# Non-local attention block: g through column tiles, and a new order of the half sums, the output projection and the peak of g

## The chip, the cores and the metric

One core of one Trainium2 chip. The metric is the time of one execution on the device in microseconds (us). The engines are TensorE (PE: matmuls; PEld: its weight loads), VectorE (DVE), ScalarE (ACT), GpSimd (POOL) and SyncE (SP), which here only issues DMAs. Each has its own queue and works it off in order; semaphores order them against each other.

## The reference

For each of 8 images x of shape 128 channels by 1024 positions:

```
g     = x^T w_g^T + b_g          (1024 x 64)
theta = x^T w_theta^T + b_theta  (1024 x 64)
phi   = w_phi x + b_phi          (64 x 1024)
att   = softmax(theta phi)       (1024 x 1024, over the last axis)
y     = att g                    (1024 x 64)
out   = x + batchnorm(w_out y + b_out)
```

## The kernel before, in words

An image has 8 tiles of 128 rows of att. The loop goes over tiles: step k issues work of several tiles at once, and every engine runs its own version of step k, written out by hand. j = k mod 8 is the *place* of a step in its image; the work of an image runs over into the next. Queues are in order, so the order of the lines of a step is the order of work. Of the 64 steps the first and last are written out singly, those between run in a loop of 16.

One tile t goes through: scores in place t-1 (TensorE, L721, four matmuls into one of two PSUM pairs of banks); row maximum (VectorE, L586, in the same place); exponential (ScalarE, L544, a place later), which frees the scores' banks for tile t+2; then turning (t+2). Tiles 0, 2, 3, 4 and 6 are turned on TensorE by eight transposes into the two banks of ps_flip (L786), read by ScalarE into an fp16 high part (pt_hi, L532) and by VectorE into a low part (pt_lo, L686); the next turned tile waits for the low part to free the bank. Tiles 1, 5 and 7 are split by GpSimd (L422, L426) and turned by DMA. VectorE corrects their row maxima by a small instruction (L591).

Four tiles are a *half*. y of a half is summed in one PSUM bank (ps_y): the *high-half matmuls* (sum_high, L733; 8 of 512 columns, 128 output rows) and two steps later the *low-half matmuls* (sum_low, L740; 8, each with 64 output rows, alternating between rows 0-63 and 64-127). The sums of the first half of an image stand in place 7 and, of the next image, 1; those of the second in 3 and 5 of the next image. VectorE then scales y (L603, places 2 and 6), TensorE projects it by w_out (convolve, L747, places 2 and 6, f32) into ps_misc, VectorE adds it to the residual (L596, places 3 and 7), SyncE stores it.

For the image after, three things are made in ps_misc too, one after the other: theta and phi (L811, places 0 and 1; ScalarE copies them out, L518), and g (project_g, L705, place 4: 8 f32 matmuls with 128 positions of x as weights and the 64 columns of w_g moving; ScalarE copies it to g_raw, L488). The largest absolute value of g sets its scale: VectorE reduces g along its rows (peak_of_g, L580, place 6), TensorE spreads the column of peaks over all partitions by a transpose (spread_peak, L727, place 7), VectorE reduces that (L655, place 0 of the next image) and derives factors (L658 to L664). GpSimd splits g into two fp16 parts (L430 to L439, place 3).

ps_misc has so many users that each waits for the last reader: the first projection of place 0 waits for the reduction of the spread peak (semaphore g_peak_read), g for the residual of place 3 (result_ready).

In a TensorE step the order before is: transposes of tile k-2; scores of tile k+1; theta and phi; output projection; g; high- or low-half matmuls; spread of the peak. On VectorE: reciprocals (places 0 and 4), scaled y, residual, peak, reduction of the spread peak, low part of tile k-2, row maximum of tile k+1.

Of the kernel before, what the change touches and what calls it, by code (L numbers as in the profile page):

```python
# [23 lines left out]
def build_nonlocal_attention(nc, x, w_tp_t, w_g_t, w_out_t, channel_vectors, out):  # L24
# [47 lines left out]
    with ExitStack() as ctx:  # L72
# [33 lines left out]
        g_raw = [sbuf(f"g_raw{i}", [P, MT, CI], F32) for i in range(2)]  # L106
# [59 lines left out]
        g_ready = sem("g_ready")  # L166
        g_out = sem("g_out")
# [96 lines left out]
        def _(sp):  # L264
# [68 lines left out]
            def image(it, k):  # L333
# [24 lines left out]
                turn_lo(MT * b + 1)  # L358
                inv_to_all(2 * b)
# [16 lines left out]
        def _(pool):  # L376
# [17 lines left out]
            def step(it, k):  # L394
# [33 lines left out]
                if j == 3 and exists(b, B) and not is_first(b):  # L428
                    hold(g_factor_ready, b + 1)
                    nc.gpsimd.tensor_scalar(out=g_parts[r][:, :, 0:CI], in0=g_raw[r][:, :, :],  # L430
                                            scalar1=g_factor[:, r:r + 1], scalar2=1.0,
                                            op0=ALU.mult, op1=ALU.mult).then_inc(g_hi_ready, 1)
                    nc.gpsimd.tensor_scalar(out=g_scaled[:, :, :], in0=g_raw[r][:, :, :],
                                            scalar1=g_factor[:, r:r + 1], scalar2=1.0,
                                            op0=ALU.mult, op1=ALU.mult).then_inc(g_scaled_ready, 1)
                if j == 3 and exists(b, B) and not is_first(b):
                    hold(g_hi_ready, b + 1)
                    hold(g_scaled_ready, b)
                    nc.gpsimd.tensor_tensor(g_parts[r][:, :, CI:2 * CI], g_scaled[:, :, :],  # L439
                                            g_parts[r][:, :, 0:CI], ALU.subtract).then_inc(g_split, 1)  # L440

                if j == 5 and exists(b + 2, B):
                    hold(g_ready, b + 2)
                    split_x(it * 16 + 16 * (k // STEPS + 2), r, 0)
                    split_x(b + 2, r, 1)
                if j == 7 and exists(b + 2, B):
                    split_x(b + 2, r, 2)

                if j == 1 and exists(b, B):
# [5 lines left out]
                    nc.gpsimd.tensor_scalar(out=resid[r][:, :], in0=x_in[r][:, :], scalar1=SHIFT, scalar2=1.0,  # L455
                                            op0=ALU.add, op1=ALU.mult).then_inc(resid_ready, 1)

# [27 lines left out]
        def _(act):  # L485
            def evacuate_g(b, source, target):
                wait(act, g_split, b - 1)
# [21 lines left out]
            evacuate_g(0, ps_flip[0][:, :], g_raw[0][:, :, :].rearrange("p t c -> p (t c)"))  # L509

            def step(it, k):
# [9 lines left out]
                if j == 5 and exists(image + 1, B):  # L521
                    act.wait_ge(g_ready, image + 2)
                    evacuate_g(image + 1, ps_misc[:, :], g_raw[(k // MT + 1) % 2][:, :, :].rearrange("p t c -> p (t c)"))
# [30 lines left out]
        def _(dve):  # L554
# [22 lines left out]
            def peak_of_g(b, r):  # L577
                dve.wait_ge(g_out, b + 1)
                wait(dve, g_peak_spread, b - 1)
                nc.vector.tensor_reduce(out=g_peak[:, r:r + 1], in_=g_raw[r][:, :, :], op=ALU.max, axis=AX.XY,  # L580
# [35 lines left out]
            def step(it, k):  # L616
# [24 lines left out]
                h = half_at(it, k - 11)  # L641
                if j % HALF_TILES == 3 and exists(h, HALVES - 2):
                    ring, part = (k - 11) // MT % 2, (k - 11) // HALF_TILES % PER_IMAGE
                    dve.wait_ge(resid_ready, image_at(it, k - 11) + 1)
                    add_residual(h, resid[ring][:, part * BANK:(part + 1) * BANK], ps_misc[:, :])
                if tile_is(it, k, 1):
                    peak_of_g(0, 0)
                if j == 6 and exists(image + 1, B):
                    peak_of_g(image + 1, (k // MT + 1) % 2)

                if j == (2 if is_first(image) else 0) and exists(image, B):
                    r = k // MT % 2
                    dve.wait_ge(g_peak_spread, image + 1)
                    spread = ps_y if is_first(image) else ps_misc
                    nc.vector.tensor_reduce(out=g_peak_all[:, r:r + 1], in_=spread[:, 0:P], op=ALU.max,  # L655
# [11 lines left out]

                if tile_is(it, k, 2):
                    dve.wait_ge(g_factor_ready, 1)
                    nc.vector.tensor_scalar(out=g_parts[0][:, :, 0:CI], in0=g_raw[r][:, :, :],  # L670
                                            scalar1=g_factor[:, 0:1], scalar2=None,
                                            op0=ALU.mult).then_inc(g_hi_ready, 1)
                if tile_is(it, k, 3):
                    dve.wait_ge(g_hi_ready, 1)
                    nc.vector.scalar_tensor_tensor(out=g_parts[0][:, :, CI:2 * CI], in0=g_raw[0][:, :, :],
# [18 lines left out]
            run_steps(dve, step)  # L694
# [6 lines left out]
        def _(pe):  # L701
# [68 lines left out]
            def step(it, k):  # L770
# [19 lines left out]

                t = tile_at(it, k + 1)
# [6 lines left out]
                if j in (0, 1) and more:  # L798
                    if j == 0:
# [4 lines left out]
                        if not is_first(image):  # L804
                            pe.wait_ge(g_peak_read, image + 1)
# [9 lines left out]
                if j % HALF_TILES == 2 and exists(h, HALVES - 2):  # L815
# [85 lines left out]
```

## Time and profile before

| | |
|---|---|
| median of 3 runs | 212.36 us (211.96 to 212.52) |
| the profiled execution | 212.18 us, of which the span is 210.4 us |
| granted clock of TensorE | 1.0 of full speed throughout |
| busy: PE / DVE / ACT / POOL | 198.5 / 178.4 / 136.8 / 152.4 us |
| DMA queue of SP | 35.01 MB, 81.2% of 16 engines |
| load of x, issue to landing | 3.3 us (median) |

The span runs from the first to the last instruction; some 1.8 us of the execution lie around it. Busy time is a sum over stages, and a busy PE counts the modelled tails of pipelined matmuls, so starts of instructions tell more than their lengths.

### The profile page before, as it was taken

The page shows a single profiled execution, that of the slowest core. Times are in us where ns is not written, and L with a number is a line of the kernel's source. Part 1 is how long each engine was busy: PE and PEld are TensorE (multiplying, and loading weights), DVE is VectorE, ACT ScalarE, POOL GpSimd, SP SyncE. Part 2 cuts the span into 40 slices and gives each one's busy share as a digit, 9 for nine tenths or more (in the row PEclk, how much of TensorE's full clock was granted, in tenths as well). Part 3 has the DMA queues.
Part 4 walks back from the last instruction along what each step waited for, and adds up shares of the span by engine and source line. Part 5 has one row for each costly group of instructions (what it writes and reads, how often), then busy time and mean ns, then how long its engine had stood idle before and what let it go on. Part 6 is the DMA issues. An engine that isn't in the chain of part 4 may idle for free.

```text
span 210.4 us, 3966 instructions
## 1 busy us (share of the span) xinstructions
PE 198.5 (94%) x1100; PEld 130.9 (62%) x1100; DVE 178.4 (85%) x291; ACT 136.8 (65%) x245; POOL 152.4 (72%) x127
## 2 busy tenths in 40 slices
PE   7996989999999998999999999999999998999993
PEld 6585856586565856577555955667565854566542
DVE  0789899978998799978999599978999699989871
ACT  2776866758575847767577666756578575658721
POOL 2448898699669998699778998699887964774400
PEclk9999999999999999999999999999999999999999
DMA  5215967999999998899959995899977997786111
GB/s 156 88 60 154 212 126 155 229 215 168 230 106 247 229 183 167 165 249 232 189 129 259 220 200 133 190 252 216 153 160 167 224 170 166 134 108 114 50 37 66
DMA packets 59500, 35.28 MB, mean 168 GB/s; under 512 B 50400, under 2 KB 50912, under 8 KB 59488
## 3 DMA queue, kind: packets, MB, share of 16 engines
q1 hardware_dynamic: 59200, 35.01, 81.2%
q10 hardware_dynamic: 288, 0.14, 0.2%
q14 instruction: 7, 0.06, 0.2%
q8 instruction: 5, 0.08, 0.2%
HBM read 8.36 MB, written 4.23 MB: 60 GB/s over the span
## 4 chain that ended last, share of the span: by engine, by line
PE 58%; DVE 15%; ACT 12%; issue 10%; DMA 2%; ACTq 1%; DVEq 0%
PE ps_scores L721 17%; PE ps_y L733 11%; PE ps_flip L786 9%; ACT probs L544 8%; PE ps_misc L705 6%; DVE neg_max L586 6%; DVE pt_lo L686 5%; PE ps_y L740 5%; ACT pt_hi L532 4%; PE ps_misc L747 3%; PE ps_misc L811 3%; DVE y_norm L603 2%; PE ps_scores L759 2%; DMA w_tp<-w_tp_t_dram 2%; PE ps_flip L705 1%
## 5 line engine op out<-in xcount | busy, mean ns | idle before, releaser
L544 ACT ACTIVATE probs<-ps_scores,neg_max 128x1024 f32<-128x1024 f32 x64 | 71.7, 1120 | 32.3 <-DVE neg_max L591 23.4
L586 DVE TENSOR_REDUCE neg_max<-ps_scores 128x1 f32<-128x1024 f32 x64 | 77.8, 1216 | 0.9 <-PE ps_scores L721 0.9
L686 DVE SCALAR_TENSOR_TENSOR pt_lo<-ps_flip,pt_hi 128x512 f16<-128x512 f32 x84 | 54.0, 685 | 15.8 <-ACT pt_hi L532 15.6
L532 ACT ACTIVATE pt_hi<-ps_flip 128x512 f16<-128x512 f32 x84 | 45.7, 596 | 20.4 <-PE ps_flip L786 20.1
L721 PE MATMUL ps_scores<-phi_hh,theta_hl 128*128 128x512 f32 x128 | 45.8, 439 | 5.2 <-ACT probs L544 4.8
L426 POOL TENSOR_TENSOR p_lo<-probs,p_hi 128x1024 f16<-128x1024 f32 x22 | 47.1, 2141 | 4.3 <-POOL p_hi L422 2.6
L786 PE MATMUL ps_flip<-ident,probs 128*128 128x128 f32 x336 | 45.0, 276 | 1.0 <-ACT probs L544 0.6
L786 PEld LDWEIGHTS ps_flip<-ident,probs 128*128 128x128 f32 x336 | 37.2, 142 | 11.6 <-issue 5.7
L721 PE MATMUL ps_scores<-phi_ll,theta_hl 128*128 128x512 f32 x128 | 40.1, 394 | 0.0
L422 POOL TENSOR_SCALAR p_hi<-probs 128x1024 f16<-128x1024 f32 x22 | 23.6, 1071 | 11.3 <-ACT probs L544 8.3
L721 PEld LDWEIGHTS ps_scores<-phi_hh,theta_hl 128*128 128x128 f32 x128 | 19.3, 190 | 18.9 <-ACT probs L544 17.5
L733 PE MATMUL ps_y<-pt_hi,g_parts 128*128 128x512 f16 (+1 forms) x128 | 30.0, 377 | 0.0
L721 PEld LDWEIGHTS ps_scores<-phi_ll,theta_hl 128*128 128x128 f32 x128 | 24.0, 188 | 5.6
L733 PEld LDWEIGHTS ps_y<-pt_hi,g_parts 128*128 128x128 f16 x128 | 11.4, 98 | 15.4 <-issue 4.2
L469 POOL TENSOR_TENSOR x_lo<-x_in,x_hi 128x512 fp32r<-128x512 f32 x14 | 17.8, 1276 | 0.8
L407 POOL TENSOR_TENSOR lo<-qk,hi 128x512 fp32r<-128x512 f32 x14 | 17.7, 1284 | 0.8
L603 DVE SCALAR_TENSOR_TENSOR y_norm<-ps_y,y_unit,inv_all 128x512 f32<-128x512 f32 x15 | 17.2, 1146 | 1.0 <-PE ps_y L740 0.9
L402 POOL TENSOR_SCALAR hi<-qk 128x1024 fp32r<-128x1024 f32 x7 | 7.4, 1051 | 13.8 <-ACT qk L518 13.8
L747 PE MATMUL ps_misc<-y_norm,wout 128*128 128x512 f32 x30 | 16.2, 620 | 0.7 <-DVE y_norm L603 0.7
L740 PE MATMUL ps_y<-pt_lo,g_parts 128*64 128x512 f16 (+1 forms) x128 | 16.7, 382 | 0.0
L705 PEld LDWEIGHTS ps_misc<-wg,x_in 128*128 128x128 f32 x112 | 13.6, 191 | 0.6
L705 PE MATMUL ps_misc<-wg,x_in 128*128 128x64 f32 x112 | 13.2, 271 | 0.0
(80 smaller groups left out, 176.8 us busy)
## 6 DMA issues: line engine op xcount, KB each, us to landing
x_in<-x_in_dram SPq DMA_DIRECT2D x16, 256.0 KB, 3.3
inv_all<-inv_row SPq DMA_DIRECT2D x15, 256.0 KB, 4.1
out_dram<-resid SPq DMA_DIRECT2D x15, 256.0 KB, 2.7
phi_hh<-hi SPq DMA_DIRECT2D x14, 256.0 KB, 5.2
phi_ll<-lo SPq DMA_DIRECT2D x14, 256.0 KB, 5.7
theta_hl<-hi SPq DMA_DIRECT2D x7, 256.0 KB, 4.3
theta_hl<-lo SPq DMA_DIRECT2D x7, 256.0 KB, 5.1
pt_hi<-p_hi SPq DMA_TRANSPOSE x22, 4.5
```

The lines of the kernel that those rows point to most:

```text
L422: nc.gpsimd.tensor_scalar(out=high[:, :], in0=p[:, :], scalar1=1.0, scalar2=0.0, op0=ALU.mult, op1=ALU.add).then_inc(p_hi_ready, 1)
L426: nc.gpsimd.tensor_tensor(low[:, :], p[:, :], high[:, :], ALU.subtract).then_inc(p_lo_ready, 1)
L532: nc.scalar.activation(pt_hi[ring][:, c * HALF_TILES:(c + 1) * HALF_TILES, slot * P:(slot + 1) * P], ps_flip[c][:, :].rearrange("p (a n) - ...
L544: nc.scalar.activation(probs[k % PROB_RING][:, :], ps_scores[k % 2][:, :], ACT.Exp, bias=neg_max[:, k % STEPS:k % STEPS + 1], accum_out=ro ...
L586: nc.vector.tensor_reduce(out=top, in_=ps_scores[k % 2][:, :], op=ALU.max, axis=AX.X, negate=True).then_inc(row_max_ready if by_dma(it, k) ...
L686: nc.vector.scalar_tensor_tensor(out=pt_lo[ring][where], in0=ps_flip[c][:, :].rearrange("p (a n) -> p a n", n=P), scalar=PROB_SCALE, in1=p ...
L705: last = nc.tensor.matmul(target[:, m * CI:(m + 1) * CI], x_in[r][:, m * P:(m + 1) * P], wg[:, :], start=True, stop=True)
L721: last = nc.tensor.matmul(ps_scores[k % 2][:, cc], theta_hl[r][:, cols], phi[:, cc], start=(n == 0), stop=(n == 1))
L733: nc.tensor.matmul(target[:, to], g_parts[r][:, m, :], pt_hi[ring][:, m, cols], start=(m == 0), stop=False, skip_group_check=True)
L740: last = nc.tensor.matmul(target[side * CI:(side + 1) * CI, to], g_parts[r][:, m, 0:CI], pt_lo[ring][:, m, cols], start=False, stop=(m >= ...
L747: nc.tensor.matmul(target, wout[:, 0:C], y_norm[:, cols], start=True, stop=True).then_inc(conv_ready, 1)
L786: last = nc.tensor.transpose(ps_flip[c][:, a * P:(a + 1) * P], probs[(k - 2) % PROB_RING][:, m * P:(m + 1) * P], ident[:, :])
```

## The change

- g is made with its channels on the partitions: two f32 matmuls with w_g as weights and 512 positions of x moving, the first into rows 0-63 of ps_misc, the second into rows 64-127 (two column tiles of the array), in place 5 behind the low-half matmuls. ScalarE copies this to g_channels, TensorE turns it back by four 128x128 transposes into ps_misc (place 6, behind the scores), ScalarE copies the result to g_raw (place 7). g_raw is one buffer instead of two, and the second copy waits for the split of the g before it.
- The high-half matmuls go ahead of the scores in their steps (places 3 and 7).
- The second output projection goes from place 6 to the end of place 7, its residual from place 7 to place 0, behind reciprocals and peak. The first projection of place 0 waits for this residual, no longer for the reduction of the spread peak.
- The peak of g goes from place 6 to place 0 of the next image, its spread to place 2 and into ps_y instead of ps_misc, the reduction to the head of place 3. The high-half matmuls of place 3, which write ps_y, wait for that reduction.
- GpSimd: input of the residual from place 1 to 3; split of g from 3 to 4; split of x from 5 to 6 (its last part stays in 7). SyncE: the store of the earlier image behind the turning DMA of a high part; the load of x behind the DMA of tile 1's low part. VectorE writes out 16 steps ahead of its loop instead of 8.

The core of the diff:

```
@@ SyncE, image(it, k)
-                store(it, k - 2 * MT + HALF_TILES)
                 inv_to_row(2 * b - 1)
                 turn_hi(MT * b - 1)
+                store(it, k - 2 * MT + HALF_TILES)
                 turn_lo(MT * b - 1)
-                if exists(b + 2, B):
-                    sp.wait_ge(g_ready, b + 1)
-                    sp.wait_ge(resid_ready, b + 1)
-                    load_x(b + 2, r)
...
                 turn_lo(MT * b + 1)
+                if exists(b + 2, B):
+                    sp.wait_ge(g_ready, b + 1)
+                    sp.wait_ge(resid_ready, b + 1)
+                    load_x(b + 2, r)
@@ ScalarE
-                wait(act, g_split, b - 1)
+                wait(act, g_split, b)
...
-                if j == 5 and exists(image + 1, B):
+                if j == 6 and exists(image + 1, B):
                     act.wait_ge(g_ready, image + 2)
-                    evacuate_g(image + 1, ps_misc[:, :], g_raw[(k // MT + 1) % 2]...)
+                    nc.scalar.activation(g_channels[:, :], ps_misc[:, :], ACT.Copy).then_inc(g_channels_out, 1)
+                if j == 7 and exists(image + 1, B):
+                    act.wait_ge(g_flipped, image + 1)
+                    evacuate_g(image + 1, ps_misc[:, :].rearrange("p (a c i) -> p a c i", c=PER_IMAGE, i=CI),
+                               g_raw[:, :, :].rearrange("p (c a) i -> p a c i", c=PER_IMAGE))
@@ VectorE, step
-                if j % HALF_TILES == 3 and exists(h, HALVES - 2):
...
-                if j == 6 and exists(image + 1, B):
-                    peak_of_g(image + 1, (k // MT + 1) % 2)
+                if j == 0 and exists(image, B) and not is_first(image):
+                    peak_of_g(image, k // MT % 2)
-                if j == (2 if is_first(image) else 0) and exists(image, B):
+                if j == (2 if is_first(image) else 3) and exists(image, B):
...
+                back = 11 if j == 3 else 12
+                h = half_at(it, k - back)
+                if j in (0, 3) and exists(h, HALVES - 2):
...
+                    add_residual(h, resid[ring][:, part * BANK:(part + 1) * BANK], ps_misc[:, :])
@@ TensorE, step, between the transposes of tile k-2 and the scores
+                h, quarter = half_at(it, k - 6), (k - 6) % HALF_TILES
+                if quarter == 1 and exists(h, HALVES - 2):
...
+                    if j == 3:
+                        pe.wait_ge(g_peak_read, image + 1)
+                    sum_high(ring, r, ps_y, slice(0, BANK), slice(0, BANK))
@@ TensorE, step, behind the scores
-                        if not is_first(image):
-                            pe.wait_ge(g_peak_read, image + 1)
+                        wait(pe, result_ready, 2 * image - 2)
...
+                if j == 2 and exists(image, B) and not is_first(image):
+                    pe.wait_ge(y_scaled, 2 * image - 1)
+                    spread_peak(image, k // MT % 2, ps_y[:, 0:P])
...
-                if j == 4 and more:
-                    pe.wait_ge(proj_out, 2 * image + 2)
-                    wait(pe, result_ready, 2 * image - 1)
-                    project_g(ps_misc, (k // MT + 1) % 2, range(MT)).then_inc(g_ready, 1)
+                if j == 6 and more:
+                    pe.wait_ge(g_channels_out, image + 1)
+                    for a in range(HALF_TILES):
+                        last = nc.tensor.transpose(ps_misc[:, a * P:(a + 1) * P],
+                                                   g_channels[:, a * P:(a + 1) * P], ident[:, :])
+                    last.then_inc(g_flipped, 1)
...
-                if j == 7 and more:
-                    wait(pe, result_ready, 2 * image)
-                    spread_peak(image + 1, (k // MT + 1) % 2, ps_misc[:, 0:P])
+                if j == 5 and more:
+                    pe.wait_ge(proj_out, 2 * image + 2)
+                    wait(pe, result_ready, 2 * image - 1)
+                    for c in range(PER_IMAGE):
+                        last = nc.tensor.matmul(ps_misc[c * CI:(c + 1) * CI, :], wg[:, :],
+                                                x_in[(k // MT + 1) % 2][:, c * BANK:(c + 1) * BANK],
+                                                start=True, stop=True, skip_group_check=True)
+                    last.then_inc(g_ready, 1)
+
+                h = half_at(it, k - 11)
+                if j == 7 and exists(h, HALVES - 2):
+                    if more:
+                        pe.wait_ge(g_out, image + 2)
...
+                    convolve(h, ps_misc[:, :], slice(0, BANK))
```

## Rows read from the trace of the kernel before

**Rows 1.** Chain of waits that ended last: shares of the span by engine.

```profile
PE 58%; DVE 15%; ACT 12%; issue 10%; DMA 2%; ACTq 1%; DVEq 0%
```

**Rows 2.** Timeline, TensorE: scores of tile 4 in images 0, 1, 7 (start, length, engine).

```profile
18.32 0.73 PE L721 MATMUL ps_scores<-phi_hh,theta_hl 128*128 128x512 f32 x2 [0.99 <-ACT probs L544]
...
40.62 0.73 PE L721 MATMUL ps_scores<-phi_hh,theta_hl 128*128 128x512 f32 x2
...
184.24 0.73 PE L721 MATMUL ps_scores<-phi_hh,theta_hl 128*128 128x512 f32 x2
```

**Rows 3.** Timeline, TensorE: a projection of image 1, places 4 to 4, images 3 and 4.

```profile
39.55 1.02 PE L747 MATMUL ps_misc<-y_norm,wout 128*128 128x512 f32 x2
39.98 0.59 PE L747 MATMUL ps_misc<-y_norm,wout 128*128 128x512 f32 x1
...
93.56 1.89 PE L705 MATMUL ps_misc<-wg,x_in 128*128 128x64 f32 x16
95.29 1.04 PE L786 MATMUL ps_flip<-ident,probs 128*128 128x128 f32 x8
...
97.19 1.05 PE L740 MATMUL ps_y<-pt_lo,g_parts 128*64 128x512 f16 x8
98.17 1.09 PE L786 MATMUL ps_flip<-ident,probs 128*128 128x128 f32 x8
99.02 0.71 PE L721 MATMUL ps_scores<-phi_hh,theta_hl 128*128 128x512 f32 x2
...
111.71 1.02 PE L747 MATMUL ps_misc<-y_norm,wout 128*128 128x512 f32 x2
113.01 0.73 PE L721 MATMUL ps_scores<-phi_hh,theta_hl 128*128 128x512 f32 x2 [0.28 <-ACT probs L544]
113.58 0.61 PE L721 MATMUL ps_scores<-phi_ll,theta_hl 128*128 128x512 f32 x2
114.04 1.90 PE L733 MATMUL ps_y<-pt_hi,g_parts 128*128 128x512 f16 x8
115.78 1.04 PE L786 MATMUL ps_flip<-ident,probs 128*128 128x128 f32 x8
```

**Rows 4.** Timeline, VectorE, the same stretch.

```profile
99.99 0.69 DVE L580 TENSOR_REDUCE g_peak<-g_raw 128x1 f32<-128x512 f32 x1
...
104.93 0.17 DVE L627 RECIPROCAL inv_sum<-row_sum 128x4 f32<-128x4 f32 x1
...
105.76 0.28 DVE L655 TENSOR_REDUCE g_peak_all<-ps_misc 128x1 f32<-128x128 f32 x1
...
107.59 1.21 DVE L586 TENSOR_REDUCE neg_max<-ps_scores 128x1 f32<-128x1024 f32 x1
...
108.94 1.22 DVE L586 TENSOR_REDUCE neg_max<-ps_scores 128x1 f32<-128x1024 f32 x1
110.08 1.13 DVE L603 SCALAR_TENSOR_TENSOR y_norm<-ps_y,y_unit,inv_all 128x512 f32<-128x512 f32 x1
111.41 1.29 DVE L686 SCALAR_TENSOR_TENSOR pt_lo<-ps_flip,pt_hi 128x512 f16<-128x512 f32 x2 [0.20 <-ACT pt_hi L532]
112.62 1.22 DVE L586 TENSOR_REDUCE neg_max<-ps_scores 128x1 f32<-128x1024 f32 x1
113.75 0.74 DVE L596 SCALAR_TENSOR_TENSOR resid<-ps_misc,bn,resid 128x512 f32<-128x512 f32 x1
114.41 1.22 DVE L586 TENSOR_REDUCE neg_max<-ps_scores 128x1 f32<-128x1024 f32 x1
115.54 0.17 DVE L627 RECIPROCAL inv_sum<-row_sum 128x4 f32<-128x4 f32 x1
```

**Rows 5.** Timeline, VectorE and TensorE, tiles 3 and 4 turned in image 0.

```profile
25.31 1.29 DVE L686 SCALAR_TENSOR_TENSOR pt_lo<-ps_flip,pt_hi 128x512 f16<-128x512 f32 x2 [0.79 <-ACT pt_hi L532]
...
26.14 1.16 PE L786 MATMUL ps_flip<-ident,probs 128*128 128x128 f32 x8 [0.18 <-DVE pt_lo L686]
...
27.06 0.71 PE L721 MATMUL ps_scores<-phi_hh,theta_hl 128*128 128x512 f32 x2
```

More of the change, by code:

```diff
@@ L105, in build_nonlocal_attention @@
         phi_ll = [sbuf(f"phi_ll{i}", [P, N], F32R) for i in range(2)]
-        g_raw = [sbuf(f"g_raw{i}", [P, MT, CI], F32) for i in range(2)]
+        g_channels = sbuf("g_channels", [P, BANK], F32)
+        g_raw = sbuf("g_raw", [P, MT, CI], F32)
         g_scaled = sbuf("g_scaled", [P, MT, CI], F32)
@@ L166, in build_nonlocal_attention @@
         g_ready = sem("g_ready")
+        g_channels_out = sem("g_channels_out")
+        g_flipped = sem("g_flipped")
         g_out = sem("g_out")
@@ L427, in step @@
                                             ALU.subtract).then_inc(p_lo_ready, 1)
[L428 to L449, printed above, removed]
+                if j == 3 and exists(b, B):
                     hold(shift_ready, 1)
@@ L456, in step @@
                                             op0=ALU.add, op1=ALU.mult).then_inc(resid_ready, 1)
+                if j == 4 and exists(b, B) and not is_first(b):
+                    hold(g_factor_ready, b + 1)
+                    nc.gpsimd.tensor_scalar(out=g_parts[r][:, :, 0:CI], in0=g_raw[:, :, :],
+                                            scalar1=g_factor[:, r:r + 1], scalar2=1.0,
+                                            op0=ALU.mult, op1=ALU.mult).then_inc(g_hi_ready, 1)
+                    nc.gpsimd.tensor_scalar(out=g_scaled[:, :, :], in0=g_raw[:, :, :],
+                                            scalar1=g_factor[:, r:r + 1], scalar2=1.0,
+                                            op0=ALU.mult, op1=ALU.mult).then_inc(g_scaled_ready, 1)
+                    hold(g_hi_ready, b + 1)
+                    hold(g_scaled_ready, b)
+                    nc.gpsimd.tensor_tensor(g_parts[r][:, :, CI:2 * CI], g_scaled[:, :, :],
+                                            g_parts[r][:, :, 0:CI], ALU.subtract).then_inc(g_split, 1)
+                if j == 6 and exists(b + 2, B):
+                    hold(proj_ready, 2 * b + 2)
+                    split_x(it * 16 + 16 * (k // STEPS + 2), r, 0)
+                    split_x(b + 2, r, 1)
+                if j == 7 and exists(b + 2, B):
+                    split_x(b + 2, r, 2)
             def split_x(count, r, part):
@@ L666, in step @@
                                             op0=ALU.mult).then_inc(y_unit_ready, 1)
+                back = 11 if j == 3 else 12
+                h = half_at(it, k - back)
+                if j in (0, 3) and exists(h, HALVES - 2):
+                    ring, part = (k - back) // MT % 2, (k - back) // HALF_TILES % PER_IMAGE
+                    dve.wait_ge(resid_ready, image_at(it, k - back) + 1)
+                    add_residual(h, resid[ring][:, part * BANK:(part + 1) * BANK], ps_misc[:, :])
                 if tile_is(it, k, 2):
                     dve.wait_ge(g_factor_ready, 1)
-                    nc.vector.tensor_scalar(out=g_parts[0][:, :, 0:CI], in0=g_raw[r][:, :, :],
+                    nc.vector.tensor_scalar(out=g_parts[0][:, :, 0:CI], in0=g_raw[:, :, :],
                                             scalar1=g_factor[:, 0:1], scalar2=None,
@@ L692, in step @@
                     row_maximum(it, k + 1)
-            run_steps(dve, step)
+            run_steps(dve, step, head=STEPS)
             dve.wait_ge(resid_ready, B)
@@ L814, in step @@
                 h = half_at(it, k - 10)
-                if j % HALF_TILES == 2 and exists(h, HALVES - 2):
+                if j == 2 and exists(image, B) and not is_first(image):
+                    pe.wait_ge(y_scaled, 2 * image - 1)
+                    spread_peak(image, k // MT % 2, ps_y[:, 0:P])
+                if j == 2 and exists(h, HALVES - 2):
                     if more:
-                        pe.wait_ge(*((proj_out, 2 * image + 2) if j == 2 else (g_out, image + 2)))
+                        pe.wait_ge(proj_out, 2 * image + 2)
                     else:
@@ L842, in step @@
                     spread_peak(0, 0, ps_y[:, 0:P])
-                if j == 7 and more:
-                    wait(pe, result_ready, 2 * image)
-                    spread_peak(image + 1, (k // MT + 1) % 2, ps_misc[:, 0:P])
+                if j == 5 and more:
+                    pe.wait_ge(proj_out, 2 * image + 2)
+                    wait(pe, result_ready, 2 * image - 1)
[8 more added lines that the diff above has]
+                        pe.wait_ge(g_out, image + 2)
+                    else:
+                        wait(pe, result_ready, h)
+                    convolve(h, ps_misc[:, :], slice(0, BANK))
                 if tile_is(it, k, TILES - 1):
```

25 lines of the change are left out of this document (9 added, 16 removed).

## The prediction

> **What bounds the kernel now.** I read the chain of waits first [rows 1]: TensorE holds 58% of the path that sets the end, VectorE 15%, ScalarE 12%. So TensorE is the first suspect, with the two others behind it in places. Next I asked whether the eight steps of an image repeat. The start of the scores of tile 4, in place 3 of the image, recurs at 40.62 us in image 1 and at 184.24 us in image 7, six images later: 143.62 us, or 23.94 us per image; from image 0 to image 1 it is 22.30 us [rows 2]. Then I read one such image on TensorE [rows 3] and on VectorE [rows 4] in order of time. TensorE issues almost without a gap: the largest in the rows is 0.28 us ahead of the scores of tile 4, where it waits for an exponential. VectorE is also nearly full between 104.93 and 115.54 us. The reader is to see that neither engine has much room: a change that makes each wait for the other once per image turns two nearly full engines, side by side, into two that run partly in turn. That is what I shall count.
>
> **Prices of what is moved** (start to start, so that pipelined tails are not counted twice). Scores of a tile 1.03 (113.01 to 114.04); high-half matmuls 1.74 (114.04 to 115.78); low-half matmuls 0.98 (97.19 to 98.17); eight transposes of a tile 0.85 (98.17 to 99.02); the old g projection 1.73 (93.56 to 95.29) [rows 3]. On VectorE: row maximum 1.13 (112.62 to 113.75), with its correction for a tile turned by DMA 1.35 (107.59 to 108.94), low part of a turned tile 1.21 (111.41 to 112.62), residual 0.66 (113.75 to 114.41), reciprocals in place 0 0.83 (104.93 to 105.76), peak of g some 0.6 (0.69 less the tail), reduction of the spread peak 0.28 [rows 4].
>
> **g itself.** It removes 1.73 us on TensorE and adds two f32 matmuls of 512 columns and four transposes. The nearest row for the matmul is the output projection: two instructions, the second starting 0.43 after the first [rows 3]. So there are four instructions of 0.43. If the two column tiles ran wholly side by side they would take 0.86, if not at all 1.72. That column tiles do overlap is in rows 3: eight low-half matmuls, alternating between the two column halves, take 0.98, where eight high-half ones of the same column count take 1.74. But here both instructions of one half are issued before both of the other, so only the middle two are neighbours on different halves; I take three times 0.43, 1.3. The transposes are half of a tile's eight, 0.43. Sum 1.73: nothing won, with ends at -0.44 and +0.42 per image.
>
> On the order of such instructions the Trainium skill has two rules: "TensorEngine Tiling (Array Packing)", Key Properties, lets different tiles run matmuls in parallel, which alone would give 0.86; "TensorE: Matmul & The Clock Gate", What overlaps and what doesn't, says that matmuls start and end strictly in program order, which gives the 1.3. No row here shows two pairs in this order, so both ends stay open; seven images of g make the difference 3 us.
>
> **One step later for g (place 4 to 5).** In place 4 g stood between the scores of tile 5 and the transposes of tile 3, and covered the time in which VectorE made the low part of tile 2, which the transposes wait for (same PSUM bank). Without the cover the wait is seen. In image 0 it once stands bare: the low part starts at 25.31, the transposes at 26.14, the next scores at 27.06 [rows 5], so the transposes can start 0.83 and the next scores 1.75 after it. Price below, in the sum.
>
> **High-half matmuls ahead of the scores (places 3 and 7).** No work is added, but the scores of tiles 4 and 0, and so their row maxima, come 1.74 later. Before, VectorE worked on those maxima while TensorE did the high half [rows 3, 4]; now it has to stand still.
>
> **The spread peak through the bank of y.** The transpose moves to place 2 and its reduction to the head of VectorE's place 3, and the high-half matmuls of place 3 (which clear that bank) get a wait for it. In the old image the output projection of place 2 starts at 111.71 and ends by 112.73; VectorE is through place 2 only at 113.75 [rows 3, 4]. Add 0.28 for the reduction and some 0.05 for the signal: TensorE would start the high half at about 114.1, 1.35 after it is free. Queued behind that wait are the scores of tile 4, and on them VectorE itself. This is the step on which the forecast rests.
>
> **Second output projection and residual (places 6 and 7 to 7 and 0).** Same work. The first projection of place 0 now waits for the residual, which on VectorE stands behind row maximum, reciprocals and peak: 1.13 + 0.83 + 0.6 + 0.66 = 3.2 after the maximum of tile 0 starts. TensorE gets there at 2.6 (from 1.18 before: scores 1.03, projection 0.86, transposes 0.85, scores 1.03), so it waits 0.6; but the maximum of tile 2, which needs the scores behind it, is not due on VectorE until 5.8, so this costs nothing on the path. Without that cover it would cost those 0.6.
>
> **ScalarE, GpSimd, SyncE.** A second copy of g, some 0.6 us like the first, lands in place 7, where ScalarE waits for VectorE; the first copy takes the place of the old one, behind g. The transposes of g wait for it, but turning tile 4 and the scores of tile 7 (0.85 + 1.03) cover it. On GpSimd residual input, g split and x split move later by one or two places, in the same order of dependence; on SyncE the load of x goes behind a turning DMA. I cost these at nothing either way. The split g is wanted by the high half of place 7, three places on. The load of x is issued at place 3 and its split stands in place 6, behind the parts of tile 5: three places of some 3 us (23.94 / 8) against a landing of 3.3 us (the profile's table). The unrolled VectorE steps cost nothing.
>
> **The sum, around the loop.** Start at the scores of tile 4. Row maximum can begin 1.18 later (113.01 to the end of the second row, 113.58 + 0.61 [rows 3]), takes 1.13, reciprocals 0.35 (0.17 in rows 4, and a scaling of like length): low part of tile 2 at 2.66. Scores of tile 6 at +1.75 [rows 5]: 4.41. Scores 1.03, low half 0.98, g 1.3, transposes of tile 4 0.85, scores 1.03, transposes of g 0.43, high half 1.74: scores of tile 0 at 11.77, its maximum at 12.95. From there VectorE is the path: 1.13 + 0.83 + 0.6 + 0.66 + 1.21 (low part, tile 6) + 1.35 + 1.14 (maxima 1 and 2) + 1.33 (scaled y with the wait behind it, 110.08 to 111.41) + 1.21 + 1.13 [rows 4] + 0.33 for the reduction and signal = 10.92. High half 1.74, and the scores of tile 4 are due again: 25.6 us, against 23.94. The stalls that this hides in TensorE are 0.8 at tile 3, 0.6 at place 0 and 1.1 at place 3; VectorE's are about 1.3 ahead of maximum 0 and 1.9 ahead of maximum 4.
>
> Five such images give 5 x 25.6 = 128.0. The last of the six has no projections and so none of the wait behind the scaled y: 25.3. Together 153.3 against 143.6: +9.7. Image 0 has no low half and no residual yet: 25.6 - 0.98 - 0.66 = 24.0 against 22.3: +1.7. Behind tile 4 of the last image 1.74 less is queued, as the high half is already done; VectorE holds the low part of tile 2 back until 2.66, so I estimate 1.4 back. Sum +10.0. The profiled execution took 212.18 (the median of the runs shown is 212.36): 222.2, and with the 0.2 between them 222.4. I round down to 222, as the wait behind y may shrink when VectorE is later.
>
> **Rivals.**
> 1. *g's column tiles don't overlap as counted.* Wholly beside each other: 0.44 less per image, 3 us, 219. Not at all (the change doesn't do what it says): +0.42, 225. For the first speaks the low half's 0.98, for the second that both instructions of one half stand together.
> 2. *Only the wait of place 3 is paid.* If the late maxima of tiles 4 and 0 find other slack, what is left per image is the bare 1.1 less the 0.28 that the scores of tile 4 no longer wait: +0.8, seven times, less 1.4 at the end, +4.4, 216.5. Against it: VectorE's rows show no such slack [rows 4].
> 3. *Faster.* TensorE stays the bound and the freed time is kept. Place: place 3, at the new wait. If VectorE reaches place 3 before TensorE ends the output projection, no stall arises, the high half fills the 0.28 that was idle, and with g at 0.86 each image costs 0.72 less: seven times, -5, 207. It decides when VectorE is 1.35 us earlier against TensorE than in the old image; for it speaks that peak and residual leave places 6 and 7, against it that they are put into place 0, ahead of place 3, on the same engine.
> 4. *No change.* Waits paid only where TensorE waited before; nothing in the rows favours it.
>
> **How the numbers follow.** Forecast with the rivals of g near it (218.5 to 225) 0.62; rival 2 and other partial cover (214 to 218.5) 0.16; above 225 0.08; within 0.3% (0.6 us, about what a measurement of this kernel tells from no change) 0.04; faster 0.10. The range from 215.5 to 226 takes in the forecast's own 218.5 to 225 (0.62), most of rival 2 (0.12) and most of what lies above (0.05). Slower by over 0.3%: 0.86.
>
> **What would show it.** A wait of the high-half matmuls in place 3 for the reduction of the spread peak, 1 us or more in each of seven images; VectorE idle ahead of the row maxima of tiles 4 and 0; transposes of tile 3 waiting for the low part of tile 2; an image of 25 to 26 us. g from its first matmul to the next transposes tells its overlap: 0.9, 1.3 or 1.7. I am wrong if VectorE reaches the reduction before TensorE asks for it.

## The result: 5.6% slower, and the profile after

The changed kernel takes 223.85 us (223.04 to 225.51, 4 runs) against 212.44 (211.96 to 212.77) for the one before on the same chip: ratio 1.056, 95% interval 1.052 to 1.059. 222.0 was forecast, with 215.5 to 226. The profiled execution took 224.01, 11.83 more than the profiled one of before. Where a kernel below had one run over 1.5% above its fastest (e4, e5, e12), its median holds that run and its ratio leaves it out.

Shares of the chain that ended last, and the busy row, after:

```profile
PE 195.6 (88%) x1044; PEld 126.0 (57%) x1044; DVE 179.2 (81%) x291; ACT 142.7 (64%) x252; POOL 152.3 (69%) x127
...
PE 53%; DVE 23%; issue 9%; SPq 4%; DMA 3%; POOL 3%; ACT 2%; DVEq 1%; POOLq 0%
```

VectorE has nearly the same work as before (179.2 us against 178.4), but its share of the path rises from 15% [rows 1] to 23%. The reader is to see that no engine got slower; engines wait for each other. The waits after (who waited for whom: us in total, times, longest us):

```profile
DVE neg_max L592 <- PE ps_scores L728: 24.6, 16, 1.9
...
POOL x_hi L466 <- DMA x_in<-x_in_dram: 11.4, 7, 3.5
...
PE ps_y L740 <- DVE g_peak_all L655: 8.0, 7, 1.4
...
PE ps_misc L828 <- POOL x_lo L471: 2.1, 1, 2.1
```

One image on TensorE, after, from place 3 to place 3 (start us, us, work, [idle before, releaser]):

```profile
94.11 1.89 PE L740 MATMUL ps_y<-pt_hi,g_parts 128*128 128x512 f16 x8 [1.10 <-DVE g_peak_all L655]
95.64 0.82 PE L728 MATMUL ps_scores<-phi_hh,theta_hl 128*128 128x512 f32 x2
...
99.18 1.25 PE L793 MATMUL ps_flip<-ident,probs 128*128 128x128 f32 x8 [0.44 <-DVE pt_lo L693]
...
102.18 1.02 PE L862 MATMUL ps_misc<-x_in,wg 128*64 128x512 f32 x4
103.14 1.09 PE L793 MATMUL ps_flip<-ident,probs 128*128 128x128 f32 x8
...
111.70 0.50 PE L828 MATMUL ps_misc<-x_hi,w_tp_hi 128*128 128x512 f32 x1 [0.79 <-DVE resid L602]
...
117.38 1.02 PE L754 MATMUL ps_misc<-y_norm,wout 128*128 128x512 f32 x2
119.49 1.89 PE L740 MATMUL ps_y<-pt_hi,g_parts 128*128 128x512 f16 x8 [1.09 <-DVE g_peak_all L655]
```

Against [rows 3], the scores of tile 4 no longer wait 0.28 for an exponential; the high half ahead of them waits 1.10 for the reduction of the spread peak. And the same image on VectorE, with a row of image 7 at the end:

```profile
96.97 1.22 DVE L592 TENSOR_REDUCE neg_max<-ps_scores 128x1 f32<-128x1024 f32 x1 [1.92 <-PE ps_scores L728]
...
108.29 1.22 DVE L592 TENSOR_REDUCE neg_max<-ps_scores 128x1 f32<-128x1024 f32 x1 [1.22 <-PE ps_scores L728]
109.43 0.17 DVE L633 RECIPROCAL inv_sum<-row_sum 128x4 f32<-128x4 f32 x1
109.63 0.77 DVE L637 TENSOR_SCALAR inv_sum<-inv_sum 128x2 f32<-128x2 f32 x1
110.31 0.68 DVE L586 TENSOR_REDUCE g_peak<-g_raw 128x1 f32<-128x512 f32 x1
...
119.06 0.28 DVE L655 TENSOR_REDUCE g_peak_all<-ps_y 128x1 f32<-128x128 f32 x1
...
184.69 2.06 DVE L637 TENSOR_SCALAR inv_sum<-inv_sum 128x2 f32<-128x2 f32 x1
```

From image 1 on, VectorE stands some 1.9 us ahead of the maximum of tile 4 in every image, and 1.22 ahead of that of tile 0 (forecast: 1.9 and 1.3).

**Where the 11.83 us are.** The scores of tile 4 start at 45.55 in image 1 and at 196.91 in image 7; before, at 40.62 and 184.24 [rows 2]. So 4.93 arise before image 1's place 3, 7.74 in the six images between (151.36 against 143.62), and 0.84 come back behind. The high half of place 3 recurs after 25.22, 24.87, 25.38, 24.87, 24.88 and 26.13 us; before, an image took 23.94.

The 4.93 lie in image 0, where the load of x came late. Its row on SyncE's queue, the split on GpSimd, and TensorE:

```profile
28.05 0.98 SPq L273 DMA_DIRECT2D x_in<-x_in_dram  x2
32.36 1.06 POOL L466 TENSOR_SCALAR x_hi<-x_in 128x1024 fp32r<-128x1024 f32 x1 [3.54 <-DMA x_in<-x_in_dram]
33.51 2.50 POOL L471 TENSOR_TENSOR x_lo<-x_in,x_hi 128x512 fp32r<-128x512 f32 x2
34.90 0.49 PE L828 MATMUL ps_misc<-x_hi,w_tp_hi 128*128 128x512 f32 x1 [2.14 <-POOL x_lo L471]
```

And the stretches of that time (from:to, length, busy us of PE, PEld, DVE, ACT, POOL, then the granted clock, DMA share, GB/s):

```profile
30.00:35.30 5.30, 3.16 (x19) 2.39 (x18) 4.26 (x7) 2.83 (x6) 2.85 (x3) 1.00 0.88 230
35.30:38.60 3.30, 3.30 (x10) 2.17 (x8) 1.44 (x3) 1.78 (x3) 3.22 (x3) 0.59 0.12 25
```

TensorE stood 2.14 us for x, and then most of 3.3 us was granted the lower level (1.2 GHz, mean 0.59).

### The profile page after: what moved, and what is told of

Read it like the earlier page. It is cut to its first block, busy times and chain, and to the rows that moved or that the text cites. A ratio compares the mean times of both kernels' runs of the same rounds, so it can differ in the third digit from the quotient of the medians.

```text
span 222.2 us, 3827 instructions
## 1 busy us (share of the span) xinstructions
PE 195.6 (88%) x1044; PEld 126.0 (57%) x1044; DVE 179.2 (81%) x291; ACT 142.7 (64%) x252; POOL 152.3 (69%) x127
## 4 chain that ended last, share of the span: by engine, by line
PE 53%; DVE 23%; issue 9%; SPq 4%; DMA 3%; POOL 3%; ACT 2%; DVEq 1%; POOLq 0%
PE ps_scores L728 14%; PE ps_y L740 12%; DVE neg_max L592 8%; PE ps_flip L793 8%; DVE pt_lo L693 7%; PE ps_y L747 6%; PE ps_misc L828 5%; DVE y_norm L609 3%; PE ps_misc L862 2%; DVE resid L602 2%; DMA x_in<-x_in_dram 2%; PE ps_scores L766 2%; DMA w_tp<-w_tp_t_dram 2%; SPq L305 1%; ACT pt_hi L538 1%
## 5 line engine op out<-in xcount | busy, mean ns | idle before, releaser
L538 ACT ACTIVATE pt_hi<-ps_flip 128x512 f16<-128x512 f32 x84 | 46.4, 595 | 31.9 <-PE ps_flip L793 31.8
L728 PE MATMUL ps_scores<-phi_hh,theta_hl 128*128 128x512 f32 x128 | 46.7, 446 | 4.4 <-ACT probs L550 4.4
L793 PE MATMUL ps_flip<-ident,probs 128*128 128x128 f32 x336 | 46.2, 278 | 4.2 <-DVE pt_lo L693 4.2
L425 POOL TENSOR_SCALAR p_hi<-probs 128x1024 f16<-128x1024 f32 x22 | 23.5, 1067 | 15.0 <-ACT probs L550 15.0
L740 PEld LDWEIGHTS ps_y<-pt_hi,g_parts 128*128 128x128 f16 x128 | 11.9, 97 | 26.2 <-issue 14.5
L728 PEld LDWEIGHTS ps_scores<-phi_hh,theta_hl 128*128 128x128 f32 x128 | 20.9, 190 | 8.6 <-ACT probs L550 5.8
L754 PE MATMUL ps_misc<-y_norm,wout 128*128 128x512 f32 x30 | 15.4, 594 | 0.5 <-DVE y_norm L609 0.5
L466 POOL TENSOR_SCALAR x_hi<-x_in 128x1024 fp32r<-128x1024 f32 x7 | 7.4, 1050 | 11.4 <-DMA x_in<-x_in_dram 11.4
L520 ACT ACTIVATE qk<-ps_misc,vec 128x512 f32<-128x512 f32 x14 | 9.6, 684 | 7.0 <-PE ps_misc L828 7.0
```

Of the source, the lines that this page charges most:

```text
L425: nc.gpsimd.tensor_scalar(out=high[:, :], in0=p[:, :], scalar1=1.0, scalar2=0.0, op0=ALU.mult, op1=ALU.add).then_inc(p_hi_ready, 1)
L538: nc.scalar.activation(pt_hi[ring][:, c * HALF_TILES:(c + 1) * HALF_TILES, slot * P:(slot + 1) * P], ps_flip[c][:, :].rearrange("p (a n) - ...
L728: last = nc.tensor.matmul(ps_scores[k % 2][:, cc], theta_hl[r][:, cols], phi[:, cc], start=(n == 0), stop=(n == 1))
L740: nc.tensor.matmul(target[:, to], g_parts[r][:, m, :], pt_hi[ring][:, m, cols], start=(m == 0), stop=False, skip_group_check=True)
L793: last = nc.tensor.transpose(ps_flip[c][:, a * P:(a + 1) * P], probs[(k - 2) % PROB_RING][:, m * P:(m + 1) * P], ident[:, :])
```

## The experiments

Theory A: the loss is the wait of the high half in place 3 for the reduction of the spread peak. Rivals: the late scores themselves (order of the high half), the late load of x, the new g, and VectorE's scaling of reciprocals. Times of before beside the runs: 211.94 to 212.05.

**Who pays: order or wait.** e1_high_behind puts the high half behind the scores again in places 3 and 7, e2_place3_behind in place 3 alone, e3_place7_behind in place 7 alone.

```
-                if quarter == 1 and exists(h, HALVES - 2):
-                    ...; sum_high(...)
                 t = tile_at(it, k + 1)
                 if exists(t, TILES):
                     scores(t, it, k + 1)
+                if quarter == 1 and j in (3, 7) and exists(h, HALVES - 2):   # e2: (3,)  e3: (7,)
+                    ...; sum_high(...)
```

> The changed kernel with the high-half matmuls behind the scores again, in places 3 and 7; all else as changed. Theory A (TensorE and VectorE work in turn: each image's loop holds both high halves, 2 x 1.5 us, in series with VectorE's chain): the loop falls to TensorE's own work of some 23.3 us per image, 211 us in all (209 to 214). Theory B (only the wait of the place-3 high half for the reduction of the spread peak costs): scores of tile 4 cover that wait, about 215. Theory C (late x, second copy of g and other data that come late; the order on TensorE is immaterial): 221 or more.

> High half behind the scores in place 3 alone, still ahead of them in place 7. A: scores of tile 4 no longer wait for high half and reduction, the loop is some 23.9 us, 214 us. B: all of the loss but the late x goes, 215, the same as with both undone. C: 221 or more.

> High half behind the scores in place 7 alone, still ahead of them, with its wait for the reduction, in place 3. A: scores of tile 0 and so VectorE's chain come 1.5 us earlier, the reduction too, so that the wait in place 3 shrinks or goes: loop 23.4 to 23.9, 212 to 215 us. B: the wait in place 3 stays, 223. C: 221 or more.

Measured: e1 216.71 (1.024, 1.020 to 1.028), e2 219.04 (1.036, 1.031 to 1.041), e3 222.81 (1.051, 1.048 to 1.053). The wait for the reduction, in e2 and in e3:

```profile
PE ps_y L740 <- DVE g_peak_all L655: 0.3, 1, 0.3
```

```profile
PE ps_y L740 <- DVE g_peak_all L655: 7.8, 7, 1.2
```

Undone in place 3, the wait is gone but for 0.3 in one image, and 4.8 us come back. Undone in place 7, it stays, 1.10 in nearly every image, and 1.0 comes back, all of it before image 1's place 3 (42.79 instead of 44.02); the six images from there take 151.3 in both kernels. So it isn't VectorE's delay by place 7 that makes the wait. But e1 stayed short of A's 211, and what its trace shows instead is the late x:

```profile
POOL x_hi L466 <- DMA x_in<-x_in_dram: 22.3, 7, 4.4
...
PE ps_misc L828 <- POOL x_lo L471: 4.6, 5, 1.6
```

**The wait taken away in another way.** e4_no_spread leaves out the spread of the peak, its reduction and the wait for images 1 to 7; the scale of g of image 0 serves for all.

```
-                    if j == 3:
-                        pe.wait_ge(g_peak_read, image + 1)
...
-                    spread_peak(image, k // MT % 2, ps_y[:, 0:P])
```

> Takes the wait itself away: images 1 to 7 use the scale of g of image 0, so the spread of the peak (transpose and reduction) is left out for them and the high half of place 3 has nothing to wait for; the order is that of the changed kernel. A: the loop loses 1.0 to 1.1 us (TensorE reaches the high half at once, but both high halves stay in series): 216 to 217. B: all of the stall goes, 213 or less. C: 222 or more.

Measured: 217.75 (1.025, 1.018 to 1.031): 6.1 back with the high half still ahead. x is late here too (GpSimd waits 16.9 us for it). From place 3 of image 4 to that of image 5, and on to image 6, this kernel takes 23.60 and 23.48, where the changed kernel takes 24.87 and 24.88; nothing but the spread with its wait differs.

**The late x.** e5_early_x is the changed kernel with the load of x ahead of the turning DMA again and the input of the residual in place 1; e11_behind_early_x adds the same to e1.

```
+                if exists(b + 2, B):
+                    sp.wait_ge(g_ready, b + 1)
+                    sp.wait_ge(resid_ready, b + 1)
+                    load_x(b + 2, r)
...
-                if j == 3 and exists(b, B):
+                if j == 1 and exists(b, B):
                     ...; nc.gpsimd.tensor_scalar(out=resid[r][:, :], in0=x_in[r][:, :], ...)
```

> The changed kernel with the input of the residual in GpSimd's place 1 and the load of x in SyncE's queue ahead of the restacking again, as before the change. Theory L (late x costs only where nothing longer hides it): in image 0 the projection of place 0 waited 2.14 us for the split x and TensorE's clock fell after it; that goes, the images after it stay as they are: 220 to 221 us. Rival M (the wait for x is itself hidden by VectorE's chain): 223.5, no change. Rival P (late x is most of the loss): 216 or less.

> High half behind the scores in both places and x early. With the high half behind alone (216.7 us) the split of x waited 22.3 us for its load in seven images and the projection 4.6 us for the split. Theory L: with the order undone late x had become the bound; both undone give 211 to 212.5 us. Rival M: x's wait was hidden; 216 to 217.

Measured: e5 223.96 (1.051, 1.047 to 1.055), no gain; e11 212.50 (1.001, 0.999 to 1.004), all of the loss gone. In e5 the total hides what the early x does. From the high half of place 7 to that of place 3, image 0 takes 12.65 us (30.32 to 42.97) instead of 15.86 (28.16 to 44.02): 3.2 less. But the residual's input now waits on GpSimd for the store (16.9 us), images of 25.83 and 25.84 appear, and the six images take 1.4 more; and in the profiled execution the first scores start at 11.37 instead of 9.16, ahead of everything that the edit moves. With the high half behind the scores the early x is worth 216.71 - 212.50 = 4.2. The two costs are in part one behind the other.

**g alone.** e7_g_alone is the kernel before with g in the new form and nothing else: column tiles in place 4, transposes in 5, copies in 5 and 6.

```
-                    project_g(ps_misc, (k // MT + 1) % 2, range(MT)).then_inc(g_ready, 1)
+                    for c in range(PER_IMAGE):
+                        last = nc.tensor.matmul(ps_misc[c * CI:(c + 1) * CI, :], wg[:, :], ...)
+                if j == 5 and more:
+                    ...; last = nc.tensor.transpose(ps_misc[:, a * P:(a + 1) * P], g_channels[...], ident[:, :])
```

> The kernel before with only g changed: two column tiles in place 4, four transposes in place 5, two copies on ScalarE. Counted on TensorE: 1.73 us go, 0.96 (as measured in the changed kernel) and 0.43 come, 0.34 less per image. Theory T (TensorE bounds each image): 2.4 us less in all, 209.5 to 210 us. Rival D (TensorE, ScalarE and VectorE bound it in turn, the last waits take the place of the work removed): 211.5 to 212.5. Rival S (the second copy on ScalarE delays the high parts behind it): slower, 213 or more.

Measured: 208.60 (0.984, 0.982 to 0.985), a little better than forecast. g on TensorE:

```profile
91.97 1.08 PE L833 MATMUL ps_misc<-x_in,wg 128*64 128x512 f32 x4
92.98 1.09 PE L793 MATMUL ps_flip<-ident,probs 128*128 128x128 f32 x8
```

1.01 from start to start, against 1.73 [rows 3]; with the transposes some 0.3 less per image, and the first five images from place 3 to place 3 are 23.45 to 23.60 us long. ScalarE's wait for g also falls, from 6.4 us in all (the copy behind the old g) to 1.5.

**The order alone.** e13_high_ahead_before is the kernel before with the high half ahead of the scores and nothing else.

> The kernel before with one part of the change alone: the high-half matmuls of places 3 and 7 ahead of the scores of their step. The spread stays in ps_misc, so no new wait comes with it. Theory A (the order by itself costs nothing, only the wait for the reduction did): 211.5 to 213. Rival B (the late scores of tiles 4 and 0 make VectorE stand and TensorE with it): some 0.8 us per image, 216 to 218.

Measured: 208.96 (0.986, 0.984 to 0.987): neither theory; the order by itself wins 3.0 us (211.95 for the kernel before beside it). The waits before, and then those of this run:

```profile
PEld ps_scores L721 <- ACT probs L544: 17.5, 22, 1.4
DVE pt_lo L686 <- ACT pt_hi L532: 15.6, 17, 1.2
```

```profile
DVE neg_max L586 <- PE ps_scores L721: 8.2, 9, 1.2
...
PEld ps_scores L721 <- ACT probs L544: 7.0, 10, 1.4
...
DVE pt_lo L686 <- ACT pt_hi L532: 5.4, 10, 0.8
```

VectorE does stand ahead of the maximum of tile 4 (0.84 to 1.17 us per image), as the prediction said. But it had stood as long one step further on, ahead of the low part of tile 2, for ScalarE. In the old image that row comes just behind those of [rows 4]:

```profile
117.04 1.29 DVE L686 SCALAR_TENSOR_TENSOR pt_lo<-ps_flip,pt_hi 128x512 f16<-128x512 f32 x2 [1.15 <-ACT pt_hi L532]
```

The idle time moved, and it shrank: the two waits of VectorE were 16.5 us (15.6, and 0.9 ahead of maxima) and are 13.6. TensorE's weight loads also wait 10.5 us less for the exponential that frees the scores' bank. Which of these makes the 3.0 wasn't separated.

**The order without the wait and with an early x.** e12_no_spread_early_x is e4 with the early x of e5; it leaves out what e4 leaves out.

> The changed kernel, high half ahead of the scores in both places, without the spread of the peak for images 1 to 7 (the scale of g of image 0 serves for all; the spread, its reduction and the wait are left out) and with the load of x and the input of the residual early. Theory A (the order of the high half costs only through the wait in place 3; with that wait and the late x gone nothing is left): 210.5 to 213, as with the high half behind the scores and an early x (212.5). Rival B (scores of tiles 4 and 0 that come 1.74 us later cost by themselves, as the prediction's step on the high half says): 215 to 218, and VectorE idle 1.2 us or more ahead of the row maxima of tiles 4 and 0 in every image with a period over 24.5.

Measured: 217.99 (1.025, 1.019 to 1.031; single runs from 215.71 to 221.17). By the total, rival B; but VectorE stands only 0.32 to 0.86 us ahead of the maxima of tile 4, short of B's 1.2, and the trace shows another reason. The high half in place 7 of image 2 and in place 3 of images 4, 5 and 6 of this run, and a wait of GpSimd:

```profile
77.69 1.90 PE L743 MATMUL ps_y<-pt_hi,g_parts 128*128 128x512 f16 x8 [2.17 <-DMA pt_hi<-p_hi]
...
118.61 1.89 PE L743 MATMUL ps_y<-pt_hi,g_parts 128*128 128x512 f16 x8
...
142.11 1.89 PE L743 MATMUL ps_y<-pt_hi,g_parts 128*128 128x512 f16 x8
...
165.58 1.89 PE L743 MATMUL ps_y<-pt_hi,g_parts 128*128 128x512 f16 x8
```

```profile
89.42 1.12 POOL L457 TENSOR_SCALAR resid<-x_in,bn 128x1024 f32<-128x1024 f32 x1 [6.02 <-DMA out_dram<-resid]
```

Two images (64.03 to 91.14 and on to 118.61, the starts of place 3) take 27.1 and 27.5: ahead of each, GpSimd waits for the store of the late second projection to land (3.22 until 61.94, 6.02 until 89.42). Its parts go out late, TensorE waits for the turned ones in place 7 (2.17 and 2.36), and the scaling of reciprocals takes 1.54 and 1.72. The wait for the store came in with this experiment's own early residual. In the two images behind them TensorE doesn't wait for turned parts: GpSimd's wait ahead of the first is 4.48, but ends (at 115.36) 3.3 us ahead of place 3, not 1.7 to 2.1. These images take 23.50 and 23.47, with the high half ahead: shorter than before's 23.94. So the run doesn't show a price of the order, and its total can't be used for one.

**The scaling of reciprocals.** The strided instruction on two columns is written as two on one column each, in the changed kernel (e6_split_scale_after), in the kernel before (e8_split_scale_before), and in e7 (e9_g_split_before).

```
-                        moved = inv_sum[:, cols.start + slots[0]:cols.start + slots[-1] + 1:2]
-                        nc.vector.tensor_scalar(out=moved, in0=moved, ...).then_inc(inv_sum_ready, 1)
+                        for slot in slots:
+                            moved = inv_sum[:, cols.start + slot:cols.start + slot + 1]
+                            scaled = nc.vector.tensor_scalar(out=moved, in0=moved, ...)
+                        scaled.then_inc(inv_sum_ready, 1)
```

> The changed kernel with VectorE's strided scaling of two reciprocals (128x2) written as two scalings of one column. In the changed kernel's trace the strided one took 0.17 to 0.77 us and 2.06 us in image 7, where it ended with a GpSimd instruction; those of one column always took 0.15. Theory S (this stands on VectorE's path to the low part of tile 2 and the maxima behind it): the period of image 7 falls from 26.1 to about 24.9, and the others by up to 0.3: 221 to 222.8. Rival H (VectorE's place is set by the scores or by GpSimd's probabilities, the scaling is covered): 223.3 to 224.2.

> The kernel before with the scaling of two reciprocals per partition in place 0 of VectorE (one instruction over 2 columns at a step of 2) made as two instructions of one column each. In the traces the one instruction ends when GpSimd's running instruction ends (0.46 to 0.91 us before the change, up to 2.06 us after it), those of one column take 0.15. Theory W (this form waits for GpSimd): the two take 0.3 together, TensorE's first projection waits less: 209.5 to 211 us. Rival V (it waits for its input, or is not on the path): no change, 211.5 to 212.5, and if its input is late the first of the two takes as long.

> The kernel before with two parts: g alone in the new form (column tiles in place 4, transposes in place 5, copies in places 5 and 6) and VectorE's strided scaling of two reciprocals written as two scalings of one column. By themselves the first gave 208.6 us and the second 211.55 against 212.05. Theory S (both remove something different, g on TensorE and ScalarE, the scaling on VectorE behind GpSimd): 208.0 to 208.4. Rival H (the scaling is hidden once g is shorter, or the extra instruction costs as much as it frees): 208.5 to 209.

Measured: e6 221.52 (1.045, 1.044 to 1.047), 2.3 back, 1.8 of it in image 7 (24.30 instead of 26.13). e8 211.55 (0.998, 0.996 to 0.999), small. e9 209.05 (0.986, 0.984 to 0.987), nothing beyond e7. In e6 the two take

```profile
184.47 0.21 DVE L638 TENSOR_SCALAR inv_sum<-inv_sum 128x1 f32<-128x1 f32 x2
```

together, against 2.06 in the same place of the changed kernel.

## Why the prediction was right, and where it wasn't

**Right: the wait of place 3.** Seven waits, 8.0 us in all, 1.10 in most images; forecast 1.1. Undoing place 3's order or leaving the spread out removes it, and e11, free of it and of the late x, is back at the old time. Its price shows where two kernels differ by the spread alone. From image 4 to 6 the changed kernel takes 24.87 and 24.88, e4 23.60 and 23.48; with x early, e5 takes 24.87 and 24.83, e12 23.50 and 23.47. That is 1.3 to 1.4 per image, some 9 to 10 us over seven as an estimate. The totals fall by only some 6, as other images then wait longer, in part for the late x (e4) or the late store (e12).

**Right: the loop, but for one stretch.** It was to run from the maximum of tile 0 through reciprocals, peak and residual and on along VectorE to the reduction. The chain that ended last does so up to the residual, and then goes through the first projection, scores and low half on TensorE and a high part on ScalarE. The forecast had called the wait of that projection free:

```profile
110.91 0.75 DVE resid L602
...
111.70 0.96 PE ps_misc L828 x3
...
114.49 0.98 PE ps_y L747 x8
115.47 0.60 PE ps_flip L793 x4
...
116.10 0.61 ACT pt_hi L538
```

The two ways are nearly of one length: the scaled y waits 0.16 to 0.31 us for the low half in each of these images. If the loop holds, an image must lengthen by what its reciprocals take. From the start of the reciprocals to the peak (109.43 to 110.31, and so in each image) it is 0.82, 0.38, 0.88, 0.39, 0.42 us in images 2 to 6, and the five periods that they end, less this, are 24.40, 24.49, 24.50, 24.48, 24.46: constant. e6, with 0.33 to 0.42 everywhere, keeps four of the five there (24.41 to 24.50). The image between 93.99 and 119.34 keeps its 25.35: its first projection waits 0.77 for the split x, for whose load GpSimd had waited 2.89. So late x stood close behind this loop. The forecast's 25.6 less its 0.83 for this part is 24.77.

**Mis-sized: g.** 1.3 was taken for the column tiles; 0.96 was measured (102.18 to 103.14). 24.77 less 0.34 is 24.43, within 0.07 of the five. That it comes out so near is in part luck. The next scores follow a high half after 1.54, where 1.74 was counted, twice; a maximum starts 1.32 after its scores, where 1.18 was counted, twice; and from the maximum of tile 0 to the next high half it is 11.20 for 10.92.

The 0.96 is near the end of the range that "TensorEngine Tiling (Array Packing)", Key Properties, of the Trainium skill alone gave (0.86 was worked out); that matmuls of one column half stand next to each other cost next to nothing.

**Mis-sized: the reciprocals.** They were counted at 0.83 in every image; three of the five periods have half of it. With g this makes the five 25.04 on average for 25.6. Image 7 has 2.17 and is 0.8 longer than the 25.3 forecast.

**Wrong: "I cost these at nothing" for GpSimd and SyncE.** The load of x was to have three places of some 3 us. In image 0 it was issued at 28.05 behind turning DMAs and a reciprocal row, and TensorE waited 2.14. Image 0 cost 4.93 where 1.7 was forecast. The 3.2 between are this wait and about 1.0 at the lower clock: the stretch from 35.69 to 38.5 is 2.8 us for work that takes 1.8 at 112.50. e5, without the wait and at a clock of 1.00, wins back 3.2 there, as shown above; the clock's share by itself wasn't tested.

**Wrong: the price of the order.** "VectorE's rows show no such slack" rested on rows that end at 115.54; 1.15 us of slack stood at 117.04. The late scores alone cost nothing and win 3.0 (e13), and without the wait images that have them take some 23.5 (two each in e4 and e12), less than before's 23.94. In place 7 beside the wait they bring nothing in all: in e3, without them, TensorE waits 0.47 ahead of the scores of tile 0 for an exponential, and the image takes 25.34 (whether its scaling takes 0.17 or 1.21) where the changed kernel's short ones take 24.87, but the changed kernel has longer ones too, and over six images the two take the same. So the delay of the maxima is paid only where the wait adds to it.

**Smaller terms.** The bare transposes of tile 3 wait 0.44 for 0.8, the first projection of place 0 up to 0.79 for 0.6. Both stand on the chain that ended last; the second was forecast to cost nothing. The end gave 0.84 back for 1.4.

So 222 was near 223.85 in part because errors cancel: the middle images 2.0 less than forecast (7.74 for 9.7), image 0 3.2 more, the end 0.6 more.

**Open.** e11 holds the gain of g and is no faster than before; its images take 24.02 where e7's take some 23.5. The waits for exponentials don't tell the two apart (17.3 us of weight loads in e11, 18.8 in e7). Late g, late projection and early residual don't by themselves hold an image at 24: e12's two quiet images have all three and take 23.50 and 23.47. Those images differ from e11's by the order of the high half and by the spread; which of the two counts wasn't separated. g and the order of the high half together, without the other parts, weren't run.

## What to carry to other kernels

A reduction that crosses from TensorE to VectorE and back into a bank that the next matmuls clear is a fixed chain; put it where TensorE has other work between, as here the kernel before did (a bank of its own wasn't tried). Before calling an engine full, read its timeline over the whole period, as idle time just outside the rows can pay for a delay inside. Parts of one change can be worth having alone: g (208.60) and the order of the high half (208.96) each beat both kernels.

## What the runs showed of the hardware

- VectorE's strided scaling of two values ends with the GpSimd instruction that is running: in the kernel before, 0.02 to 0.04 us behind its end in all seven images; in five images of e1 no GpSimd instruction ran, and it took 0.17. In the changed kernel's image 7 it ended at 184.69 + 2.06 = 186.75, and this at 184.58 + 2.14 = 186.72:

```profile
184.58 2.14 POOL L429 TENSOR_TENSOR p_lo<-probs,p_hi 128x1024 f16<-128x1024 f32 x1
```

  Written as one column each, the 22 of e6 took 0.143 to 0.156 us. This agrees with the exclusive lock between VectorE and GpSimd that the Trainium skill describes ("SBUF — State Buffer", Who interferes with whom); that it is this lock was not tested further.
- Four f32 matmul instructions of 512 columns, two on one column half and then two on the other, take 0.96 (changed kernel) to 1.01 us (e7) to the next work's start, where two on the full width take 0.86 (108.09 to 108.95 in the changed kernel).
- After a wait of 2.14 us of TensorE the granted clock of the next 3.3 us was 0.59, with 1.00 before it; with an early x (e5, e11) it stayed at 1.00 there. In the same place it was 0.61 behind waits of 2.16 (e6) and 2.04 (e4) and 0.66 behind 1.99 (e2), and stayed at 1.00 behind waits of 1.83 (e3) and 1.56 (e1).
